# First mixed tile's x loaded ahead of the last stores, and its strip products moved behind the third and fourth down product

## What is computed

```python
x = x + attn(cond(x, style), w_qkv, q_ln, k_ln, w_out)      # 32 heads, causal, ALiBi bias
y = einsum('bsi,boi->bso', x, W[adapter])                    # one of 8 adapter matrices 512x512 per batch
h = relu(einsum('bsh,hi->bsi', y, up_w)) ** 2                # 512 -> 1024
shared = einsum('bsi,ih->bsh', h, down_w)                    # 1024 -> 512
routed = einsum(y -> fc1 -> expert -> fc2) * sum(top2(y @ gate_w))
x = x + layernorm(shared + routed) * gamma + beta
```

## Time and profile before

| | |
|---|---|
| median of 3 runs | 1122.14 us (1119.28 to 1123.42) |
| the profiled execution: its own time | 1117.33 us |
| its span, first to last instruction | 1115.5 us |
| PE busy | 1068.9 us, 96% of the span |
| DVE, ACT, POOL busy | 622.4, 570.1, 565.3 us |
| mean granted TensorE clock | 0.991 of full speed |

### The profile page before, as it was taken

How to read it: one execution, slowest core, us unless ns; L and a number is a source line. 1 busy time by engine, 2 the same in 40 slices (tenths; PEclk the granted TensorE clock), 3 DMA queues, 4 the chain that set the end, 5 groups by cost and what they waited for, 6 DMA issues and landing times.

```text
span 1115.5 us, 28260 instructions
## 1 busy us (share of the span) xinstructions
PE 1068.9 (96%) x11412; PEld 848.4 (76%) x11412; DVE 622.4 (56%) x1050; ACT 570.1 (51%) x955; POOL 565.3 (51%) x490
## 2 busy tenths in 40 slices
PE   5999999999999999999989599999999999999994
PEld 3878888888887888888778476777878787787883
DVE  4677767676766677666765124444544534454432
ACT  3576777777777777777775203424060514232220
POOL 5666877777776767776745112323242323233331
PEclk9999999999999999999999899999999999999998
DMA  6225454555545455555477927443526253130101
GB/s 255 62 79 174 170 185 162 185 167 181 176 171 187 160 187 188 193 159 182 144 263 263 349 89 219 168 95 128 147 71 198 63 192 91 39 85 29 48 29 38
DMA packets 99984, 166.52 MB, mean 149 GB/s; under 512 B 45648, under 2 KB 46416, under 8 KB 96016
## 3 DMA queue, kind: packets, MB, share of 16 engines
q1 hardware_dynamic: 90304, 140.97, 38.5%
q0 software_dynamic: 6064, 17.05, 5.2%
q10 hardware_dynamic: 3488, 6.70, 1.8%
HBM read 98.09 MB, written 40.89 MB: 125 GB/s over the span
## 4 chain that ended last, share of the span: by engine, by line
PE 87%; DMA 3%; issue 3%; POOL 2%; DVE 2%; ACT 1%; SPq 1%; ACTq 0%; DVEq 0%; POOLq 0%
PE pair L934 15%; PE banks L910 15%; PE banks L701 14%; PE bank L750 7%; PE bank L701 7%; PE bank L814 7%; PE bank L927 4%; PE banks L927 4%; PE bank L691 3%; PE pair L718 3%; PE pair L778 2%; PE banks L830 2%; DMA xm<-x_rows 1%; PE banks L880 1%; PE banks L761 1%
## 5 line engine op out<-in xcount | busy, mean ns | idle before, releaser
L1774 POOL TENSOR_TENSOR w_lo<-w2t,w_hi 128x2048 fp32r<-128x2048 f32 x26 | 119.5, 4595 | 70.5 <-ACT w_hi L1101 70.5
L1839 POOL TENSOR_TENSOR u_lo<-act,u_hi 128x512 fp32r<-128x512 f32 x64 | 82.5, 1289 | 124.3 <-ACT u_hi L1313 124.3
L1863 POOL TENSOR_TENSOR frstd<-fve,cst 128x1 f32<-128x1 f32 x32 | 31.9, 996 | 195.9 <-DVE fve L1707 195.9
L1700 DVE TENSOR_TENSOR total<-total,pair 128x512 f32<-128x512 f32 x32 | 22.0, 688 | 168.5 <-PE pair L934 168.5
L701 PE MATMUL banks<-wqkv_hi,h_hi 128*128 128x512 f32 x256 | 103.4, 404 | 0.7 <-DVE wqkv_lo L1575 0.5
L910 PE MATMUL banks<-yT_hi,up_hi 128*128 128x512 f32 x256 | 101.4, 396 | 0.0
L1646 DVE TENSOR_TENSOR act<-act 128x512 f32<-128x512 f32 x59 | 63.0, 1068 | 66.8 <-ACT act L1309 66.8
L701 PE MATMUL banks<-wqkv_hi,h_lo 128*128 128x512 f32 x256 | 99.9, 390 | 0.0
L701 PE MATMUL banks<-wqkv_lo,h_hi 128*128 128x512 f32 x256 | 99.9, 390 | 0.0
L910 PE MATMUL banks<-yT_hi,up_lo 128*128 128x512 f32 x256 | 99.8, 390 | 0.0
L910 PE MATMUL banks<-yT_lo,up_hi 128*128 128x512 f32 x256 | 99.7, 389 | 0.0
(11 more groups left out here) (208 smaller groups left out, 2888.6 us busy)
## 6 DMA issues: line engine op xcount, KB each, us to landing
w2t<-in_w SPq DMA_DIRECT2D x26, 1024.0 KB
w<-in_w SPq DMA_DIRECT2D x24, 768.0 KB
vx<-v_hl SPq DMA_DIRECT2D x128, 68.0 KB
x1g<-x_rows SPq DMA_DIRECT2D x32, 256.0 KB, 2.7
kx<-k_hl SPq DMA_DIRECT2D x124, 64.0 KB
x_rows<-x1t SPq DMA_DIRECT2D x31, 256.0 KB, 2.4
y_rows<-ys SPq DMA_DIRECT2D x26, 256.0 KB
w<-in_w SPq DMA_DIRECT2D x24, 256.0 KB, 2.9
```

The costliest lines, as they stand in the source:

```text
L1774: e.tensor_tensor(w2_lo[:, :, :], w2t[:, :, :], w2_hi[:, :, :].bitcast(F32), ALU.subtract).then_inc(d_wlo, 1)
L1839: e.tensor_tensor(u_lo[n % FC][:, :], act[n % 2][:, :], u_hi[n % FC][:, :].bitcast(F32), ALU.subtract) \
```

## The change

```diff
@@ load_mixed
                 if k:
                     e.wait_ge(d_y[(t - 1) % 2], 16 * ((t - 1) // 2 + 1))
+                else:
+                    e.wait_ge(a_store[t % 2], 16 * (t // 2 + 1))
                 e.dma_start(xm[:, :], x1_rows[P * t:P * t + P, :]).then_inc(x_rows, 16)
@@ SP, end of the attention phase
             store_x1(T - 2)
+            load_mixed(0)
             upto(e, "o", T - 1)
             fetch_down(down_lo, 1, 0, FC - 1)
@@ SP, loop over the groups
                 if m == 0:
                     load_first(0)
-                    load_mixed(0)
                     upto(e, "r", T - 1)
                     load_back(1, 0, 0, KC)
                     load_back(1, 1, 0, KC)
+                if m == 0:
+                    load_x1(2)
                 if mixed_in(m):
                     load_last(m)
                     if m == 0:
-                        load_x1(2)
                         load_x1(3)
                     store_mixed(m)
                     if mixed_in(m + 1):
+                        load_mixed(m + 1)
                         load_first(m + 1)
                 if m:
                     load_x1(GROUP * m + 2)
                     load_x1(GROUP * m + 3)
-                if mixed_in(m + 1):
-                    load_mixed(m + 1)
                 if m + 2 < GROUPS:
                     load_y(m + 2)
@@ PE, behind down(m, t)
-                    if m == 0 and t == 0:
-                        e.wait_ge(S["relu"], FC)
+                    if m == 0 and t == 2:
                         adapt_first(0, B3)
-                    if m == 0 and t == 2:
-                        adapt_last(0, B3)
+                if m == 0:
+                    adapt_last(0, B3)
@@ ACT, behind the scaling of tile t
-                    if m == 0 and t == 2:
+                    if m == 0 and t == GROUP - 1:
                         mixed_out(0, B3)
```

## The result

| | before | after |
|---|---|---|
| median of 13 runs | 1121.41 us (1119.28 to 1123.42) | 1116.05 us (1111.82 to 1120.49) |
| ratio after to before | | 0.9953, 95% interval 0.9939 to 0.9967 |
| the profiled execution's own span | 1115.5 us | 1114.2 us |

The account below looks back on a forecast made before the run. PE, busy 96% of the span, was taken as the bound, with waits for xm. 12.4 us won up to E, half given back in group 1, leaves 6.0: 1122.14 - 6.0 = 1116.1 us, range 1112.0 to 1120.4.

Parts of the forecast that it names:

- The wait ahead of group 0's downs: Before down(0, 0): loading xm of tile 26 early removes 11.35 us of PE waiting; slow clock behind it costs about 1.3 us.
- F: Start of the transposes of tile 26, or PE's coming free for them; 626.37 in the profile before.
- The new wait in SP: Group 1's loads queue behind the ym store, landing 2.4 us after issue at E + 3.5; strip loads issue from E + 4.9.
- E: End of adapt_last(0) in group 0, forecast at 666.25, with 12.4 us won up to there.
- The wait for the strips: Before adapt_first(1): strip loads take 11 us, landing at E + 15.9, a PE wait of 5.9 us.
- what sets `up(1, 5)`: In group 1: y transfers, then ACT's relu of product 3, let up(1, 5) start at E + 25.9; gain 6.0 us.
- the strip path: In group 1: strip wait, 1.3 us of slow clock, strip and up products; up(1, 4) ends at E + 25.4.
- the short wait at `up(1, 5)`: Sign in group 1: PE waits 0 to 2 us for ACT at an up product.
- The y transfers do not bind: Rival in group 1: strips land at E + 13.5 and alone set the pace; gain 9 us, 1113.1 us, chance 0.13.
- No second wait: Rival in group 1: strips land before E + 10, all 12.4 us stay; 1109.7 us, chance 0.07.
- slower: Rival in group 1: three or more further y-transfer stalls; three make it 2 us slower, 1124.2 us, chance 0.05.
- The later groups: From group 2: SP's wait for the ym store, some 2.4 us, lies below four down products; cost 0.

Follow-up runs that it names:

- y_early: The change, with the y transfers of group 2 issued right behind load_back instead of behind group 1's strip loads; 1115.64 us, ratio 0.9942 to the kernel before.
- warm_y_early: The change, with group 2's y transfers early and 22 unused products ahead of adapt_first(1); 1113.96 us, ratio 0.9935 to the kernel before.
- products_alone: The kernel before, with only the strip products moved behind the third and fourth down (and load_x1(2) moved), xm not early; 1130.44 us, ratio 1.0092.
- xm_behind: The change, with load_mixed(m + 1) put back behind the strip loads, xm of tile 26 still early; 1117.80 us, ratio 0.9971 to the kernel before.
- keep_warm: The change, with 22 unused products of 5 us in all on PE ahead of adapt_first(1); 1115.52 us, ratio 0.9951 to the kernel before.

## Why the prediction was right, and where not

**The wait ahead of group 0's downs.** Right. `xm` landed 11.0 us after its issue at 611.55, some 8 us before PE came to it, the granted clock stayed at 1.00, and PE did not wait for `down_lo`. (The price of the old slow clock was put at 1.3 us; the two windows named give 1.4. And the wait itself was that of one execution, see above.) From F to the end of `adapt_last(0)` I had 39.9 us (666.25 - 626.37); it was 670.22 - 630.86 = 39.4. The 0.4 us for `gate_products(1)` was not paid, and the last strips were hidden below `down(0, 3)`, as assumed.

**The new wait in SP.** I had the `ym` store land 2.4 us after its issue, from x1's stores; it was 2.0. The first strip load was issued at E + 4.3 in place of 4.9.

**The wait for the strips.** I had it end at E + 15.9; it ended at 686.05 - 670.22 = E + 15.8. That is two errors that cancel: the loads started 0.6 us sooner and took 11.6 us to the end of the wait in place of 11. I had a wait of 5.9 us; it was 6.6, since PE got there 0.7 us sooner, `xm` having cost only 0.3 us in place of 1.

**The step that failed: what sets `up(1, 5)`.** I took the y transfers and ACT's relu, at E + 25.9, with the strip path just below, at E + 25.4. The relu was ready at E + 25.1 (695.29 - 670.22), inside my bounds of 24.5 to 27.2; the strip path came at E + 26.6 and set the end, and the short wait at `up(1, 5)` that I had named as a sign did not appear. The term that was mis-sized is the clock: 1.3 us, taken from the low windows of before, against 2.5 us measured (5.26 - 2.78). In the old wait, products were granted full clock again about 3 us after PE had resumed; here the clock stayed low for nearly the whole of the strip products, 5 us. The trace of `y_early` confirms that the y transfers did not bind, and that of `warm_y_early` that the clock did; the times alone show neither. The sum came out near (6.0 against 5.8 in the traces and 5.4 in the medians) because two paths lay within 1.5 us of each other; a part of its closeness is luck. So is that of the absolute time (1116.1 forecast, 1116.05 measured): the gain was 0.6 us smaller and the median it was taken from 0.7 us too high. The range had a flaw, too. Its upper end, 7.8 us, takes the y path at E + 24.5, but by the prediction's own strip path `up(1, 5)` could not start before E + 25.4, which caps the gain at 698.15 - (665.9 + 25.4) = 6.9 us.

**The rivals.** "The y transfers do not bind" was true of the mechanism, but its 9 us needed the strips at E + 13.5, and they came at 15.8. "No second wait" and "slower" did not occur; that the move of the products can make the kernel slower is shown by `products_alone`. I had no rival in which one half of the change works against the other, though the sum contained it: 12.4 us won up to group 1, half of it given back. What I had not asked is whether a place one down earlier would keep both.

**The later groups.** Right: behind the gate products of group 1 the two programs run alike, with no wait of PE of 0.3 us or more in either, and take 408.1 us in both. The wait for the store took SP 2.1 us in group 2 (709.70 to 711.78), under cover, as forecast.

**Memory bandwidth.** The window from 682 to 684 after the change moved 409 GB/s, again above the 358 GB/s of the Trainium skill's page "DMA: Bandwidth & Descriptors", section "Specifications"; the traces of this kernel do not show that limit.

## What to carry to other kernels

When work is moved later to spare a wait for its input, look up what hangs on its end: here four strip loads, a store and the next load were all released by the last strip product, and putting that off by one down product cost more than half of what the early load had won (7.7 of 11.7 us in the traces). There is often a place between: load the input early, and put the work just behind the point at which its input is surely there (here one down earlier, 13 to 15 us in place of 5 won). And before comparing two profiled executions, line them up at a point ahead of the change: here 4.5 us of the difference lay in a phase in which the change adds one load and which varied by as much without it.

## What was not expected of the hardware

- The granted clock was low for about 3 us after one wait (11.35 us, followed by the transposes and the down products) and for about 5 us after a shorter one (6.6 us, followed by the strip products); in `products_alone`, behind a wait of 8.7 us, it was low for 6 us, and one up product took 5.06 us in place of 2.73. The price in clock was about 1.4 us for the first, 2.5 for the second and 2.8 for the third, and about 1.7 behind the 9.5 us of `xm_behind`: not in the order of the waits' lengths. Why isn't known.
- The same 256 KB store of `ym` landed 2.0 to 2.1 us after its issue in eight traces, and after 4.2 to 4.4 us in three (`keep_warm`, `xm_behind`, `products_alone`). Why isn't known.
